# A two-block recurrent and attention kernel: normalised rows turned by 32x32 blocks and a DRAM exchange in place of TensorE transposes

## The reference, cut to what matters

```
xn = layernorm(x)
s  = xn + rmsnorm(recurrent(xn), norm_w)          # a linear map of the rows here
g  = silu(fwht(silu(xn W1^T) * (xn W3^T)) W2^T)
x  = x + s * g

xn = layernorm(x)
z  = (xn - mean(xn)) / sqrt(var(xn) + 1e-5) * gamma + beta
s  = softmax(causal(z Wq (z Wk)^T / 16)) (z Wv) Wo + xn
g  = silu(fwht(silu(xn W1^T) * (xn W3^T)) W2^T)
x  = x + s * g
```

## Time and profile before

| | us |
|---|---|
| median of 3 executions | 383.63 |
| lowest, highest | 382.83, 383.70 |
| profiled execution | 383.55 |
| its span, first to last instruction | 381.8 |
| TensorE busy within the span | 374.7 (98%) |
| VectorE busy | 235.4 (62%) |
| ScalarE busy | 158.3 (41%) |
| GpSimd busy | 87.6 (23%) |

### The profile page before, as it was taken

One profiled execution on the slowest core, in us unless ns is written; L12 is line 12 of the kernel. 1 busy time (PEld: TensorE's weight loads), 2 busy tenths in 40 slices (PEclk: granted clock), 3 DMA queues, 4 the chain that ended last, 5 costly groups with the idle time before them and its releaser, 6 DMA issues.

```text
span 381.8 us, 5244 instructions
## 1 busy us (share of the span) xinstructions
PE 374.7 (98%) x1961; PEld 319.3 (84%) x1961; DVE 235.4 (62%) x469; ACT 158.3 (41%) x311; POOL 87.6 (23%) x111
## 2 busy tenths in 40 slices
PE   6999999999999999999999999999999999999996
PEld 3888888878888888888988988888888888888885
DVE  5589973596358736785457954479443795334832
ACT  2654451444135512551374513644236352354410
POOL 1143510153013201266304220024200152000302
PEclk9899999999999999999999999999999999999999
DMA  7993000120012001000010000101001010010101
GB/s 229 296 356 107 2 1 7 47 86 2 0 49 91 1 0 44 14 3 0 21 36 1 2 0 14 43 0 57 0 8 47 3 57 0 2 48 7 57 0 55
DMA packets 21248, 17.08 MB, mean 45 GB/s; under 512 B 5092, under 2 KB 20712, under 8 KB 21224
## 3 DMA queue, kind: packets, MB, share of 16 engines
q1 hardware_dynamic: 21224, 16.76, 14.3%
HBM read 10.98 MB, written 2.10 MB: 34 GB/s over the span
## 4 chain that ended last, share of the span: by engine, by line
PE 94%; DVE 3%; DMA 1%; SPq 1%; issue 0%; ACT 0%; DVEq 0%
PE GU L257 18%; PE GU L259 18%; PE GU L258 18%; PE O L257 9%; PE O L259 8%; PE O L258 8%; PE T L264 5%; PE GU L264 1%; DMA stage<-in_L_ffn_W 1%; PE O L264 1%; PE O L333 1%; PE T L257 1%; PE T L258 1%; PE T L259 1%; DVE hf L796 1%; DVE hid L717 1%
## 5 line engine op out<-in xcount | busy, mean ns | idle before, releaser
L606 ACT ACTIVATE hf<-GU 128x512 f32<-128x512 f32 x64 | 38.2, 598 | 87.7 <-DVE hid L717 51.0
L796 DVE TENSOR_TENSOR hf<-hf,GU 128x512 f32<-128x512 f32 x64 | 43.9, 685 | 48.1 <-PE GU L259 41.7
L257 PE MATMUL GU<-XT,W1T 128*128 128x512 f32 x128 | 51.3, 400 | 0.0
L257 PE MATMUL O<-hid,W2hi 128*128 128x512 f32 (+1 forms) x128 | 50.2, 392 | 0.0
L259 PE MATMUL GU<-XT,W1T 128*128 128x512 f32 x128 | 50.0, 391 | 0.0
L258 PE MATMUL GU<-XT,W1T 128*128 128x512 f32 x128 | 50.0, 390 | 0.0
L257 PE MATMUL GU<-XT,W3T 128*128 128x512 f32 x128 | 49.9, 390 | 0.0
L259 PE MATMUL GU<-XT,W3T 128*128 128x512 f32 x128 | 49.9, 390 | 0.0
L258 PE MATMUL GU<-XT,W3T 128*128 128x512 f32 x128 | 49.8, 389 | 0.0
L259 PE MATMUL O<-hid,W2lo 128*128 128x512 f32 (+1 forms) x128 | 49.1, 384 | 0.0
L258 PE MATMUL O<-hid,W2hi 128*128 128x512 f32 (+1 forms) x128 | 49.1, 383 | 0.0
(11 more groups left out here) (187 smaller groups left out, 706.6 us busy)
## 6 DMA issues: line engine op xcount, KB each, us to landing
stage<-in_L_ffn_W SPq DMA_DIRECT2D x24, 256.0 KB, 4.9
sT<-GX SPq DMA_DIRECT2D x112, 32.0 KB, 1.9
X<-in_L_attn_x SPq DMA_DIRECT2D x1, 1536.0 KB, 9.1
out<-X SPq DMA_DIRECT2D x3, 512.0 KB, 2.9
wqkv<-in_L_attn_qkv SPq DMA_DIRECT2D x1, 768.0 KB
X<-in_L_attn_x SPq DMA_DIRECT2D x2, 256.0 KB, 2.9
win<-in_L_attn_W_in SPq DMA_DIRECT2D x1, 512.0 KB
wout<-in_L_attn_W_out SPq DMA_DIRECT2D x1, 512.0 KB
```

The source lines that it names most:

```text
L257: pe.matmul(o, lhs(0), rhs(0), start=start, stop=False)
L606: act.activation(hf[:, c % 2, :], GU[:, c % 2, 0, :], ACT.Silu).then_inc(silu_done, 1)
L796: dve.tensor_tensor(hf[:, c % 2, :], hf[:, c % 2, :], GU[:, c % 2, 1, :], ALU.mult).then_inc(mul_done, 1)
```

## The change

The eleven blocks of eight transposes go from TensorE. `x_turn(n)` turns the normalised rows by 32x32 blocks on VectorE into `GX`, directly behind `normalise`. SP moves them by `move_rows`: one DMA (`scatter`, 512 KB) to a scratch tensor in DRAM, a wait, and four DMAs (`gather`, 128 KB each) into `sT`. `x_hi` (ScalarE) and `x_lo` (now GpSimd) make the parts of `XT` from `sT`. The gate goes the same way, one scatter and four gathers instead of 16 DMAs. For z, `spread_c2` sends the factors through DRAM and reads them back into every partition (`c2B`); VectorE's `scale_z` multiplies `sT` by this table, ScalarE applies gamma and beta, then rounds, and GpSimd subtracts.

`sT` and `GX` now hold the rows and the gate by turns, with waits: the gate's silu waits for `xt_ready` and `z_scaled`, `gate_flip` for `rows_out`, `x_turn` for `gate_out`. In block 1 `stats` stands behind chunk 0, `gate_product` behind chunk 1, `normalise` and `x_turn` behind chunk 4. `ZT`, `zfull` and `c2B` lie where the first block's weights were, so the first `c2B` waits for the end of block 0's up projections.

```diff
+            def scatter(scratch, done):
+                sp.dma_start(scratch.rearrange("j p f -> p j f"), GX[:, :, :, :, :].rearrange("p j t k a -> p j (t k a)")).then_inc(done, 16)
+            def gather(scratch, done):
+                for j in range(QUADS):
+                    sp.dma_start(turned[j * Q:(j + 1) * Q].rearrange("p i t k a -> p i (t k a)"),
+                                 scratch[j].rearrange("(i b) f -> b i f", i=QUADS)).then_inc(done, 16)
             def move_gate(n):
                 sp.wait_ge(gate_flipped, 2 * n + 2)
-                for i in range(QUADS):
-                    for j in range(QUADS):
-                        sp.dma_start(gate_rows[j * Q:(j + 1) * Q, i, :, :, :].rearrange("p t k a -> p (t k a)"),
-                                     GX[i * Q:(i + 1) * Q, j, :, :, :].rearrange("p t k a -> p (t k a)")).then_inc(gate_moved, 16)
+                scatter(swap_gate, gate_out)
+                sp.wait_ge(gate_out, 16 * n + 16)
+                gather(swap_gate, gate_moved)
+            def move_rows(n):
+                sp.wait_ge(rows_turned, 2 * n)
+                scatter(swap_rows, rows_out)
+                sp.wait_ge(rows_out, 16 * n)
+                gather(swap_rows, rows_moved)
+            def spread_c2(m):
+                sp.wait_ge(c2_ready, m + 1)
+                sp.dma_start(c2_line.rearrange("(t p) -> p t", p=P), c2[:, :], allow_slow_non_contiguous=True).then_inc(c2_out, 16)
+                sp.wait_ge(c2_out, 16 * m + 16)
+                if m == 0:
+                    sp.wait_ge(up_done, NB * HC)
+                sp.dma_start(c2B[:, :], c2_line.rearrange("(a r) -> a r", a=1).broadcast_to([P, ROWS])).then_inc(c2_in, 16)
...
             def block1_group(n, prev_layer):
                 m = n - NB
-                if prev_layer == 1:
-                    pe.wait_ge(pt_ready, 3 * m)
-                x_transposes(n)
                 if prev_layer == 0:
                     pe.wait_ge(u_ready, 2 * PAIRS)
-                for i in range(2):
-                    down_chunk(prev_layer, n - 1, i)
-                pe.wait_ge(z_ready, m + 1)
-                pe.wait_ge(mul_done, 8 * n)
-                for k in range(KC):
-                    transposes(GU[:, 1, k, :], [PZ[:, t * D + k * P:t * D + (k + 1) * P] for t in range(TILES)]).then_inc(zt_tr, 1)
-                for i in range(2, 6):
+                for i in range(6):
                     down_chunk(prev_layer, n - 1, i)
                 pe.wait_ge(zt_ready, 2 * m + 2)
...
+            def x_turn(n):
+                dve.wait_ge(xn_ready, n + 1)
+                if n > 1:
+                    dve.wait_ge(gate_out, 16 * (n - 1))
+                for k in range(KC):
+                    dve.transpose(rows_gx[:, :, k, :].rearrange("p j (t b) -> p t j b", t=TILES),
+                                  rows2[n % 2][:, :, k * P:(k + 1) * P].rearrange("p t (j a) -> p t j a", j=QUADS)).then_inc(rows_turned, 1)
+            def scale_z(n):
+                m = n - NB
+                dve.wait_ge(c2_in, 16 * m + 16)
+                dve.wait_ge(rows_moved, 64 * n)
...
             def gate(n):
+                act.wait_ge(xt_ready, 2 * n + 4)
+                if n >= NB - 1:
+                    act.wait_ge(z_scaled, 2 * (n - NB) + 4)
```

More of the change, by code:

```diff
@@ L104, in two_block_kernel @@
             vR = sb("vR", [P, 2, TILES, D], F32R, early)
+            ZT = sb("ZT", [P, 2, KC, ROWS], F32R, early)
+            zfull = sb("zfull", [P, KC, ROWS], F32, early)
+            c2B = sb("c2B", [P, ROWS], F32, early)
         W1T0 = sb("W1T0", [P, 2, KC, H], F32R)
@@ L153, in two_block_kernel @@
         stage_loaded = [[sem(f"stage{i}_loaded{w}") for w in range(3)] for i in (0, 1)]
-        out_stored, gate_moved = sem("out_stored"), sem("gate_moved")
+        out_stored, gate_moved, gate_out = sem("out_stored"), sem("gate_moved"), sem("gate_out")
+        rows_turned, rows_out, rows_moved, c2_out, c2_in = sem("rows_turned"), sem("rows_out"), sem("rows_moved"), sem("c2_out"), sem("c2_in")
+        z_scaled = sem("z_scaled")
+        swap_gate, swap_rows = (nc.dram_tensor(f"swap_{x}", [QUADS, P, TILES * KC * Q], F32).ap() for x in ("gate", "rows"))
+        c2_line = nc.dram_tensor("c2_line", [ROWS], F32).ap()
         w_tr, w2_tr, w_hi, w_lo = sem("w_tr"), sem("w2_tr"), sem("w_hi"), sem("w_lo")
@@ L353, in small_av, with first_x_transposes @@
                 last.then_inc(sm_mm, 1)
-            def x_transposes(n, bank=T):
-                pe.wait_ge(xn_ready, n + 1)
+            def first_x_transposes():
+                pe.wait_ge(xn_ready, 1)
                 for k in range(KC):
-                    transposes(bank[:, k, :], [rows2[n % 2][:, t, k * P:(k + 1) * P] for t in range(TILES)]).then_inc(xt_tr, 1)
+                    transposes(GU[:, 1, k, :], [rows2[0][:, t, k * P:(k + 1) * P] for t in range(TILES)]).then_inc(xt_tr, 1)
             def up_chunk(l, n, c, first):
@@ L499, in block1_group @@
                 pe.wait_ge(t_ready, 2 * m + 2)
[L500 removed]
+                pe.wait_ge(mul_done, 8 * n)
+                if prev_layer == 1:
+                    pe.wait_ge(pt_ready, 3 * m)
                 for i in range(TILES):
@@ L674, in block1_group @@
                 for k in range(KC):
-                    hi(zT[0][k], sT[:, k, :], zfull_ready, 2 * m + k + 1, zt_hi)
+                    act.wait_ge(z_scaled, 2 * m + k + 1)
+                    act.activation(zfull[:, k, :], zfull[:, k, :], ACT.Identity, scale=gb[:, 0, k:k + 1], bias=gb[:, 1, k:k + 1]).then_inc(zfull_ready, 1)
+                for k in range(KC):
+                    hi(zT[0][k], zfull[:, k, :], zfull_ready, 2 * m + k + 1, zt_hi)
                 act.wait_ge(tail_used, n)
@@ L832, in between_chunks @@
                         pair_u(1, PAIRS + 1, 1)
-                if c == 1 and not last:
+                if c == (1 if n < NB else 0) and not last:
                     stats(n + 1, ((n + 1) % NB) * TILES)
-                if c == 6 and not last:
+                if c == (6 if n < NB else 4) and not last:
                     dve.wait_ge(combined, 4 * n)
                     normalise(n + 1, ((n + 1) % NB) * TILES)
+                    x_turn(n + 1)
             def recurrent_scale(n):
@@ L910, in block0_group @@
                 hid_lo_chunk(n, HC - 1)
[L912 to L920, removed]
-                last.then_inc(z_ready, 1)
             def block1_group(n, prev_layer, last=False):
@@ L925, in block1_group @@
                 if prev_layer == 0:
-                    second_norm(n)
-                    x_lo(n)
+                    recurrent_scale(n - 1)
+                    scale_z(n)
                 else:
                     attention_scale(n - 1)
-                dve.wait_ge(prod_ready, 4 * n - 4)
-                for k in range(KC):
-                    dve.wait_ge(zt_tr, 2 * m + k + 1)
-                    dve.tensor_scalar(sT[:, k, :], GU[:, 1, k, :], gb[:, 0, k:k + 1], gb[:, 1, k:k + 1], ALU.mult, ALU.add)\
-                       .then_inc(zfull_ready, 1)
-                if prev_layer == 0:
-                    recurrent_scale(n - 1)
-                else:
-                    x_lo(n)
                 for j in range(KC):
@@ L1030, in second_norm, with x_lo @@
                 pool.tensor_tensor(c2[:, :], ctmp[:, :], mhalf[:, :], ALU.pow).then_inc(c2_ready, 1)
+            def x_lo(n):
+                for k in range(KC):
+                    pool.wait_ge(xt_hi, 2 * n + k + 1)
+                    pool.tensor_tensor(xT[1][k].rearrange("p (t q b) -> p t q b", t=TILES, q=QUADS), rows_at[:, :, k, :].rearrange("p q (t b) -> p t q b", t=TILES),
+                                       xT[0][k].bitcast(F32).rearrange("p (t q b) -> p t q b", t=TILES, q=QUADS), ALU.subtract).then_inc(xt_ready, 1)
             def rms_of(n):
@@ L1072, in block1_group @@
                     rstd_of(n + 1)
+                    second_norm(n + 1)
                 add_to_x(n - 1, x_at)
-                if not last:
-                    second_norm(n + 1)
             def m_is_first(m):
```

68 lines of the change are left out of this document (48 added, 20 removed).

## The result

| | before | after |
|---|---|---|
| median, us | 383.66 | 390.41 |
| lowest, highest | 382.83, 384.20 | 389.53, 391.27 |
| profiled execution | 383.55 | 390.25 |
| its span | 381.8 | 388.4 |
| TensorE busy | 374.7 | 367.2 |

The ratio is 1.018, with a 95% interval of 1.016 to 1.020: slower by 6.8 us, where 382.2 was forecast and 387.0 was the upper end of the range.

What follows compares the result with a forecast made beforehand. TensorE, busy 374.7 of 381.8 us, was taken to bound the kernel. 383.55 - 9.7 (transposes) + 0.6 (head) + 6.1 (group 4 wait) + 1.7 (clock) = 382.25, forecast 382.2 us, range 378.5 to 387.0.

Steps and rivals of the forecast that it cites:

- The transposes: Starts of groups on TensorE: removing the transposes of rows and of `PZ` saves 9.7 us, all on the path.
- The factors' write: Group 4, c2 to DRAM ahead of the table's read: 2.0 us, by the 32 KB row.
- The table's read: Group 4, `c2B` read from DRAM, 256 KB, behind the factors' write: 3.0 us.
- 6.1 at group 4: TensorE's wait for `zt_ready`: arrival at 177.0, ready at 183.2, so 6.1 us; range 4 to 8.5.
- Rival B: Hops through DRAM cost more than their rows, kernel slower than before; 5 us more make 388; chance 0.20.
- Groups 5 to 7 at no cost: Starts of block 1's later groups: 1.2 us of slack at the tightest, 4 to 5, so no wait.
- The clock: Behind group 4's wait TensorE's granted clock falls, costing 1.7 us (0 to 3).
- The head: Group 1: the turn on VectorE delays the weights' preparation, so TensorE waits 0.6 us (0 to 1.3).
- No waits at groups 2 and 3: Starts of groups 2 and 3: rows ready with 2.1 us of slack, 1.1 with slower gathers, cost nothing.
- none for the gate: Gate's scatter and gathers take 6.5 us after the flip; 6 us of slack before `gate_product`, cost nothing.
- 2.8 us for the scatter: Rows' scatter to DRAM, priced like a store of the output: 2.9 us to landing, 3.0 with SP's reaction.
- The gathers: Four reads of rows into `sT`, issued 0.5 us apart; one lands in 2.0 us, ends 1.9 and 3.0.

Runs made afterwards that it cites:

- kernel with no new wait: Changed kernel with group 4's factors sent early in 16-byte pieces, table product before recurrent scaling, block 0's gate product and turn two chunks earlier: 374.47 us, ratio 0.9758.

## Why the prediction was wrong, point by point

**The transposes: right.** 9.7 us were to go. The kernel with no new wait is 9.3 us faster than before. Groups of block 1 take 47.4 us there from one first `ZT` matmul to the next; before it was 49.2 (178.80 to 228.02), less 1.76 by the forecast's sum.

**The factors' write: the step that failed.** Priced 2.0 us by a row of 32 KB in long pieces; it took 6.6. The forecast called it its least known term, and still gave it no more than 1 us above its row (its 8.1 us of wait, with 1 us more for each of the two hops): the row it leaned on has pieces hundreds of times as long. The same write in sixteen-byte pieces took 2.2 us, near the 2.0. The Trainium skill, "DMA: Bandwidth & Descriptors", section Specifications, which the forecast cited, warned in the right direction (below 512 B a transfer turns into read-modify-write), but for the time to landing the step isn't there: alone, 64 and 16 bytes take 2.2 to 2.9 us here, and only 8 and 4 bytes more. The measurement decides.

**The table's read: mis-sized.** 3.0 by the row of 256 KB; 4.1 to 5.0 in the kernel after. About half of that at group 4, 0.9 of 1.7, goes with the four-byte pieces by the run with sixteen. With the write, 4.6 + 1.7 = 6.3 us, which is the 12.2 instead of 6.1 at group 4. Rival B, at 0.20, named this mechanism; its 5 us more for the hops made 388, and with the groups behind it the kernel went past even that.

**Groups 5 to 7 at no cost: wrong.** The forecast gave them 1.2 us of slack behind a write of 2 us. It took 8.0 to 10.1 there, and SP stands at it, so that the rows' scatter leaves late, and beside the read and the store: the term put at nothing was the queue behind the write. SP's timeline in group 6:

```profile
258.64 0.38 SPq L236 DMA_DIRECT2D c_line<-c  x1
268.77 0.34 SPq L240 DMA_DIRECT2D c2B<-c_line  x1
269.16 0.44 SPq L286 DMA_DIRECT2D out<-X  x1
269.64 0.51 SPq L211 DMA_DIRECT2D swap_rows<-GX  x1
275.56 1.74 SPq L216 DMA_DIRECT2D sT<-swap_rows  x4
```

The read, the store and the scatter leave within 0.9 us, and the scatter takes 5.9 us instead of 2.8. The first `ZT` matmuls of groups 4 to 7 stand at 186.90, 236.30, 285.15 and 332.96: 49.40, 48.85 and 47.81 apart, over 47.43 in the kernel with no wait. Less the clock's 1.7 in the first, that is 0.3, 1.4 and 0.4: 2.1 us.

**The clock: right.** TensorE's windows (us, busy, instructions, granted clock, DMA share, GB/s), from the wait on:

```profile
181.00:186.80 5.80, 0.00 (x0) 0.50 0.00 1
186.80:192.00 5.20, 5.10 (x15) 0.65 0.00 0
192.00:198.00 6.00, 6.00 (x37) 1.00 0.23 82
```

The clock fell to 1.2 GHz (0.50) in the wait and came back behind it: 5.2 x 0.35 = 1.8 us, forecast 1.7 (0 to 3). The first mix matmul with `VR` is 11.5 us behind the first on `ZT`, 9.8 in the kernel with no wait: 1.7 again. The closeness is in part luck, as the loss doesn't go by the length of the wait: measured the same way in the other runs it was 2.9 us behind the wait of 13.5, 2.3 behind 7.6, 1.4 behind 5.8, 2.3 behind 4.6 and 2.5 behind 3.6.

**The head: mis-sized, small.** 0.6 was forecast for group 1; it was some 0.1. VectorE's timeline:

```profile
39.97 1.30 DVE L848 STREAM_TRANSPOSE GX<-rows 128x512 f32<-128x512 f32 x2
41.19 0.65 DVE L868 TENSOR_TENSOR hf<-hf,GU 128x512 f32<-128x512 f32 x1
41.77 2.31 DVE L769 TENSOR_TENSOR hid<-hf,hid 128x512 fp32r<-128x512 f32 x1
44.00 1.21 DVE L791 TENSOR_TENSOR U<-U 128x1024 f32<-128x1024 f32 x1
```

As argued, the standing still of 3.42 us gave way to the turn; it is now in the subtraction into `hid`, but only to the end of GpSimd's own. The sum ends at 45.21, 0.2 us later than before (45.00), not 0.7.

**No waits at groups 2 and 3, none for the gate, 2.8 us for the scatter: right.** The gathers took 2.5 instead of 2.0, inside the forecast's ends (1.9 and 3.0).

**One figure of the forecast is off by itself.** A wait of 4 us at group 4 makes 383.55 - 9.7 + 0.6 + 4 + 1.7 = 380.15 by its own terms, not 379.9. Nothing hangs on it.

**The sum with measured terms:** 383.55 - 9.7 + 0.1 + 12.2 + 1.7 + 2.1 = 389.95; the execution took 390.25. The same sum gives 383.55 - 9.7 + 0.1 + 7.6 + 2.3 = 383.85 for the sixteen-byte pieces (384.27), 380.8 without factors (381.53) and 374.0 with no wait (374.47).

## What to carry over

Price a DMA by a row with its piece length, not with its bytes alone, and give a term that no row covers a wide upper end; here the layout of 512 factors decided between slower and equal. Look also at who reads the new layout: it cost VectorE 0.8 us a group. When an operation is taken off the engine that bounds a kernel and given to a chain of hops, the gain comes only if the chain starts early enough: look for the earliest place at which its first step can stand, and move that, before shortening the hops. A queue's order is part of a transfer's price, since what stands behind a slow one pays as well.

## What the runs showed of the hardware

A write to DRAM of 512 pieces of 4 bytes took 6.6 to 11.3 us (the 11.3 from SP's next issue), and one of 128 pieces 6.8 to 7.3; 8 bytes took 4.1 to 4.6, and 16 or 64 bytes 2.2 to 2.9 alone, 16 bytes 1.4 to 3.2 within the kernels. A 512 KB scatter that was issued 0.46 us behind a write in 4-byte pieces took 11.75 us instead of 2.8, and 3.5 behind one in 16-byte pieces. A line just written in 4-byte pieces was read into all partitions in 3.6 to 5.1 us, in 4.1 or more in all cases but one; one written in 16-byte pieces in 3.0 to 3.8. A VectorE product of 128x512 float32 took 1.08 us with the table read four elements apart, and 0.69 with it read in order. TensorE's granted clock was 0.50 to 0.72 over the 5 to 6 us behind waits of 3.6 to 13.5 us, which cost 1.4 to 2.9 us, not in the order of the waits' lengths.
